# Layer 2 attention of a four-layer kernel: scores as wide products with the mask added on TensorE, and the passes as a loop on each engine

## The reference

```python
q_in = x @ Wq.T                                   # _L2_attn_ref, x already normed
qkv = (q_in @ Wqkv.T + bqkv).reshape(Bs, Ls, 3, Ds)
q, k, v = ...                                     # each (Bs, Ls, G=4 heads, dh=32)
scores = einsum('blgd,bmgd->bglm', q, k) * scale
h = relu(q_in) @ Wop.T
dx_g = (sigmoid(h @ W2.T + b2) * Ls)[:, None] + windows[None, :, None, None]
masked = where(win_mask > dx_g, -BIG, scores)     # win_mask: distance, huge above the diagonal
attn = softmax(masked + scores)
out = einsum('bglm,bmgd->blgd', attn, v)
# _L2_ffn_ref, on the same x
h = silu(lin(x, w1)) * lin(x, w2)
h = gelu(lin(h, h1)); h = gelu(lin(h, h2)); return lin(h, w3)
```

## Time and profile before

| | |
|---|---|
| median of 3 runs | 2189.82 us (2189.76 to 2194.12) |
| the profiled execution | 2189.82 us, span 2188.0 us |
| mean granted TensorE clock | 0.958 |
| layer 2's eight passes | 1216.7 to 1624.1 us |

### The profile page before, as it was taken

How to read it: one execution, slowest core, us unless ns; L and a number is a source line. 1 busy time by engine, 2 the same in 40 slices (tenths; PEclk the granted TensorE clock), 3 DMA queues, 4 the chain that set the end, 5 groups by cost and what they waited for, 6 DMA issues and landing times.

```text
span 2188.0 us, 47512 instructions
## 1 busy us (share of the span) xinstructions
PE 1984.2 (91%) x15804; PEld 1520.2 (69%) x15804; DVE 1491.9 (68%) x5508; ACT 1144.1 (52%) x3575; POOL 901.4 (41%) x1415
## 2 busy tenths in 40 slices
PE   5887887399999999999999899999979999999998
PEld 2555654278887778888777566666657777777776
DVE  6989963366666666666666655556657777777776
ACT  3444352155555555555555454455546666666665
POOL 3113266354554454455445311111125545545544
PEclk9888799699999999999999999999989999999999
DMA  6000016600000000000000000000000000000001
GB/s 189 16 2 1 2 40 168 177 1 2 2 1 2 2 1 1 2 2 1 2 2 1 1 1 1 1 1 1 1 1 2 2 2 1 2 2 2 2 2 40
DMA packets 40592, 37.19 MB, mean 17 GB/s; under 512 B 5664, under 2 KB 38560, under 8 KB 39456
## 3 DMA queue, kind: packets, MB, share of 16 engines
q1 hardware_dynamic: 34720, 29.82, 4.3%
q0 software_dynamic: 5632, 4.33, 1.4%
HBM read 23.53 MB, written 10.62 MB: 16 GB/s over the span
## 4 chain that ended last, share of the span: by engine, by line
PE 56%; DVE 10%; ACT 9%; issue 4%; POOL 3%; DMA 0%; DVEq 0%; POOLq 0%; ACTq 0%
PE bank L1318 7%; PE bank L1307 6%; PE bank L1246 5%; PE bank L1293 5%; PE bank L1290 4%; PE bank L1340 3%; ACT work L1378 3%; PE bank L1231 2%; PE bank L1233 2%; PE bank L1232 2%; PE bank L1310 2%; ACT work L1379 2%; PE bank L1239 2%; PE bank L1786 1%; PE bank L1715 1%
## 5 line engine op out<-in xcount | busy, mean ns | idle before, releaser
L1609 POOL TENSOR_TENSOR work<-work 128x128 f32<-128x128 f32 (+1 forms) x1048 | 506.5, 514 | 659.3 <-DVE work L1526 659.3
L1378 ACT ACTIVATE work<-work 128x128 f32<-128x128 f32 x524 | 206.9, 395 | 513.9 <-DVE work L1514 513.9
L1521 DVE COPY work<-bank 128x384 f32<-128x384 f32 x520 | 283.5, 549 | 21.5 <-PE bank L1318 6.5
L1379 ACT ACTIVATE work<-work 128x256 f32<-128x256 f32 x524 | 258.7, 494 | 0.0
L1318 PE MATMUL bank<-w_const,work 128*128 128x128 f32 x1560 | 227.6, 282 | 1.0 <-POOL work L1609 1.0
L1514 DVE CUSTOM_DVE_ANT_0 work<-bank,mask 128x256 f32<-128x256 f32 x524 | 219.6, 419 | 0.0
L1318 PEld LDWEIGHTS bank<-w_const,work 128*128 128x128 f32 x1560 | 165.8, 141 | 46.2 <-issue 41.8
L1513 DVE CUSTOM_DVE_ANT_0 work<-bank,mask 128x128 f32<-128x128 f32 x524 | 150.5, 287 | 52.3 <-PE bank L1293 48.3
L1307 PE MATMUL bank<-work 128*64 128x256 f32 x1032 | 168.4, 403 | 4.7 <-DVE work L1547 4.3
L1547 DVE COPY work<-bank 128x512 f32<-128x512 f32 x136 | 93.4, 687 | 112.7 <-PE bank L1241 79.4
L1231 PE MATMUL bank<-l_xn_hi,l_qk_hi 128*128 128x256 f32 x532 | 163.4, 307 | 3.0 <-DVE l_xn_lo L1442 2.8
(11 more groups left out here) (335 smaller groups left out, 4883.0 us busy)
## 6 DMA issues: line engine op xcount, KB each, us to landing
w_l<-in_l SPq DMA_DIRECT2D x1, 3210.5 KB, 11.8
w_l<-in_l SPq DMA_DIRECT2D x2, 1540.0 KB, 7.5
w_f<-in_f SPq DMA_DIRECT2D x1, 3072.0 KB, 14.3
x_sb<-in_x SPq DMA_DIRECT2D x4, 512.0 KB, 5.8
normed_rows<-work SPq DMA_DIRECT2D x1, 2048.0 KB, 9.3
even_experts<-x_sb SPq DMA_DIRECT2D x8, 256.0 KB, 3.6
residual<-x_sb SPq DMA_DIRECT2D x1, 2048.0 KB, 9.8
qk<-in_qk SPq DMA_DIRECT2D x2, 1024.0 KB, 8.2
```

The lines of the kernel that those rows point to most:

```text
L1378: act.activation(pr[g % 4][:, Q0], pr[g % 4][:, Q0], ACT.Exp, scale=-1.0, bias=nmx[:, g % 4, 0:1], accum_out=sm[:, g % 4, 0:1])
L1379: act.activation(pr[g % 4][:, Q1], pr[g % 4][:, Q1], ACT.Exp, scale=-1.0, bias=nmx[:, g % 4, 1:2], accum_out=sm[:, g % 4, 1:2]).then_inc(s ...
L1521: dve.tensor_copy(pt[g % 4], PS[2 + g % 2][:, 0:384]).then_inc(s_te.s, 1)
L1609: ins = pool.tensor_tensor(w, w, spread(rc[:, g % 4, q:q + 1], w.shape[1]), ALU.mult)
```

## The change

It touches `layer2()` alone.

- Scores: `kT` becomes `kb`, four blocks of 512 columns, block g with head g's k on its own 32 partitions and zeros elsewhere (POOL writes the zeros once, before the passes). A product of all 128 rows of `qT` with two blocks then gives two heads' scores side by side in one bank. Ahead of them a product of the bf16 unit matrix with the bf16 mask tiles puts the mask into the same bank. A set of scores is six products of 512 columns in banks 0 to 2.
- ACT fills `kb` with four activations of 32 partitions in place of one of 128.
- `maxima` becomes three plain reductions of the banks; `exps` reads the banks. What waited for the end of the maxima, because they had read the banks, waits for the exps now. PE's scores wait for the masks.
- Order: on DVE `masks(1)` and `stats` stand ahead of `maxima(0)`; on PE the turn of x stands ahead of `scores(1)`.
- Banks: the transposes use 3 and 4, the values 5, two middle products 5 and 3, with the waits that belong to them.
- On PE, ACT, DVE and POOL `for i in range(PASSES)` becomes `with engine.Fori(0, PASSES) as i`: one body, run eight times with a branch at its end, each wait's value and the addresses of x's tiles computed in registers.

```diff
-            kT = carve(512)
+            kb = carve(G2, 512)
...
-            MID_BANKS = ((6, 7, 4, 5), (6, 7, 0, 1))
-            TURN_BANKS = (5, 4)
+            MID_BANKS = ((6, 7, 5, 3), (6, 7, 0, 1))
...
-                pe.wait_ge(pre_k, 1)
+                pe.wait_ge(pre_k, 2)
                 pe.wait_ge(pre, 4)
-                for i in range(PASSES):
+                with pe.Fori(0, PASSES) as i:
...
                             if layer == 0 and c == 2:
-                                pe.wait_ge(m_e.s, m_e.at(i, place["k"]))
+                                pe.wait_ge(ot.s, ot.at(i, -1))
+                                pe.wait_ge(d_e.s, d_e.at(i, 0))
                             if layer == 0 and c == 3:
-                                pe.wait_ge(d_e.s, d_e.at(i, 0))
                                 pe.wait_ge(t_e.s, t_e.at(i, -1))
                             if layer == 1 and c == 2:
-                                pe.wait_ge(s_mx.s, s_mx.at(i, 1))
+                                pe.wait_ge(s_ex.s, s_ex.at(i, 1))
...
                     def scores(p):
-                        pe.wait_ge(s_mx.s, s_mx.at(i, p - 1))
-                        if p == 0:
-                            pe.wait_ge(dv.s, dv.at(i, GATED_3))
-                            pe.wait_ge(o_e.s, o_e.at(i, -1))
-                            pe.wait_ge(ot.s, ot.at(i, -1))
-                        for g in range(G2):
-                            r = slice(DH2 * g, DH2 * (g + 1))
-                            pe.matmul(PS[g][:, 0:256], qT[r, p * 256:p * 256 + 128], kT[r, p * 256:(p + 1) * 256], start=True, stop=True, skip_group_check=True)
...
+                        pe.wait_ge(mb_s.s, mb_s.at(i, p))
+                        pe.wait_ge(s_ex.s, s_ex.at(i, p - 1))
+                        pe.wait_ge(o_e.s, o_e.at(i, -1))
+                        for j in range(2):
+                            pe.matmul(PS[j][:, :], ident16[:, :], mb0[p][:, 2 * j:2 * j + 2, :].rearrange("p g k -> p (g k)"), start=True, stop=False)
+                        pe.matmul(PS[2][:, :], ident16[:, :], mb1[p].rearrange("p g k -> p (g k)"), start=True, stop=False)
+                        for j in range(2):
+                            pe.matmul(PS[j][:, :], qT[:, p * 256:p * 256 + 128], kb[:, 2 * j:2 * j + 2, p * 256:(p + 1) * 256], start=False, stop=True)
+                        pe.matmul(PS[2][:, :], qT[:, p * 256 + 128:(p + 1) * 256], kb[:, :, p * 256 + 128:(p + 1) * 256],
+                                  start=False, stop=True).then_inc(s_f.s, 1)
...
-                    scores(1)
-                    pe.wait_ge(f_ig.s, f_ig.at(i, 2))
                     pe.wait_ge(ln_x.s, ln_x.at(i, 0))
                     turn()
+                    scores(1)
...
-                    act.activation(kT, PS[4][:, :], ACT.Identity, bias=L["bk"]).then_inc(m_e.s, 1)
+                    for g in range(G2):
+                        r = slice(DH2 * g, DH2 * (g + 1))
+                        ins_ = act.activation(kb[r, g, :], PS[4][r, :], ACT.Identity, bias=L["bk"][r, :])
+                    ins_.then_inc(m_e.s, 1)
...
+                        act.wait_ge(t_f.s, t_f.at(i, 4 * p + 3 - 8))
                         for g in range(G2):
-                            act.activation(pr0[p][:, g, :], pr0[p][:, g, :], ACT.Exp, scale=-1.0, bias=nmx[:, p, 0, g:g + 1],
+                            act.activation(pr0[p][:, g, :], PS[g // 2][:, g % 2 * 256:(g % 2 + 1) * 256], ACT.Exp, bias=nmx[:, p, 0, g:g + 1],
...
+                    masks(1)
+                    tile = 4 * i + 4
+                    stats(i, tile)
                     def maxima(p):
-                        dve.wait_ge(mb_s.s, mb_s.at(i, p))
                         dve.wait_ge(s_f.s, s_f.at(i, p))
-                        dve.wait_ge(t_f.s, t_f.at(i, 4 * p + 3 - 8))
-                        for g in range(G2):
-                            dve.tensor_tensor_reduce(pr0[p][:, g, :], PS[g][:, 0:256], mb0[p][:, g, :], -1.0, BIG, ALU.add, ALU.min, nmx[:, p, 0, g:g + 1])
...
+                        for j in range(2):
+                            dve.tensor_reduce(nmx[:, p, 0, 2 * j:2 * j + 2], PS[j][:, :].rearrange("p (g k) -> p g k", k=256), AX, ALU.max, negate=True)
+                        dve.tensor_reduce(nmx[:, p, 1, :], PS[2][:, :].rearrange("p (g k) -> p g k", k=128), AX, ALU.max, negate=True).then_inc(s_mx.s, 1)
...
             def pool_(pool):
+                pool.memset(kb, 0.0).then_inc(pre_k, 1)
```

More of the change, by code:

```diff
@@ L1766, in turned @@
                         for c, src in enumerate((pr0[p][:, g, 128:256], pr1[p][:, g, :], pr0[p][:, g, 0:128])):
-                            mm = pe.transpose(PS[TURN_BANKS[n % 2]][:, c * 128:(c + 1) * 128], src, ident)
+                            mm = pe.transpose(PS[(3, 4)[n % 2]][:, c * 128:(c + 1) * 128], src, ident)
                         mm.then_inc(t_f.s, 1)
@@ L1772, in values @@
                         pe.wait_ge(ot.s, ot.at(i, p - 1))
-                        pe.wait_ge(s_mx.s, s_mx.at(i, 1))
                         for g in range(G2):
                             r = slice(DH2 * g, DH2 * (g + 1))
-                            pe.matmul(PS[3][r, 0:256], v_sb[:, 2 * p + 1, r], pt[g][:, 0:256], start=True, stop=False, skip_group_check=True)
+                            pe.matmul(PS[5][r, 0:256], v_sb[:, 2 * p + 1, r], pt[g][:, 0:256], start=True, stop=False, skip_group_check=True)
                         for g in range(G2):
                             r = slice(DH2 * g, DH2 * (g + 1))
-                            pe.matmul(PS[3][r, 0:128], v_sb[:, 2 * p, r], pt[g][:, 256:384], start=False, stop=True,
+                            pe.matmul(PS[5][r, 0:128], v_sb[:, 2 * p, r], pt[g][:, 256:384], start=False, stop=True,
                                       skip_group_check=True).then_inc(pv.s, 1)
@@ L1849, in act_ @@
                 act.activation(xnT, PS[4][:, :], ACT.Copy).then_inc(m_e.s, 1)
-                act.wait_ge(pre_k, 1)
-                for i in range(PASSES):
+                act.wait_ge(pre_k, 2)
+                with act.Fori(0, PASSES) as i:
                     def silu(c):
@@ L1869, in act_ @@
                     act.wait_ge(m_f.s, m_f.at(i, place["k"]))
-                    act.activation(kT, PS[4][:, :], ACT.Identity, bias=L["bk"]).then_inc(m_e.s, 1)
+                    for g in range(G2):
+                        r = slice(DH2 * g, DH2 * (g + 1))
+                        ins_ = act.activation(kb[r, g, :], PS[4][r, :], ACT.Identity, bias=L["bk"][r, :])
+                    ins_.then_inc(m_e.s, 1)
                     def exps(p):
                         act.wait_ge(s_mx.s, s_mx.at(i, p))
+                        act.wait_ge(t_f.s, t_f.at(i, 4 * p + 3 - 8))
                         for g in range(G2):
-                            act.activation(pr0[p][:, g, :], pr0[p][:, g, :], ACT.Exp, scale=-1.0, bias=nmx[:, p, 0, g:g + 1],
+                            act.activation(pr0[p][:, g, :], PS[g // 2][:, g % 2 * 256:(g % 2 + 1) * 256], ACT.Exp, bias=nmx[:, p, 0, g:g + 1],
                                            accum_out=sm[:, p, 0, g:g + 1])
-                            ins_ = act.activation(pr1[p][:, g, :], pr1[p][:, g, :], ACT.Exp, scale=-1.0, bias=nmx[:, p, 1, g:g + 1],
+                        for g in range(G2):
+                            ins_ = act.activation(pr1[p][:, g, :], PS[2][:, g * 128:(g + 1) * 128], ACT.Exp, bias=nmx[:, p, 1, g:g + 1],
                                                   accum_out=sm[:, p, 1, g:g + 1])
@@ L1900, in head_out @@
                 act.wait_ge(pv.s, pv.at(i, 4 * p + 3))
-                act.activation(oT[:, p * 256:(p + 1) * 256], PS[3][:, 0:256], ACT.Identity, bias=L["bv"]).then_inc(ot.s, 1)
+                act.activation(oT[:, p * 256:(p + 1) * 256], PS[5][:, 0:256], ACT.Identity, bias=L["bv"]).then_inc(ot.s, 1)
             def dve_(dve):
@@ L1948, in dve_ @@
                 dve.sem_inc(pre_k, 1)
-                for i in range(PASSES):
+                with dve.Fori(0, PASSES) as i:
                     k[0] = 0
@@ L2008, in turned_out @@
                             dve.wait_ge(pv.s, pv.at(i, n - G2))
-                            dve.tensor_copy(pt[n % G2], PS[TURN_BANKS[n % 2]][:, 0:384]).then_inc(t_e.s, 1)
+                            dve.tensor_copy(pt[n % G2], PS[(3, 4)[n % 2]][:, 0:384]).then_inc(t_e.s, 1)
                     maxima(0)
-                    masks(1)
-                    tile = 4 * i + 4
-                    stats(i, tile)
                     moments()
@@ L2039, in pool_ @@
                     pool.tensor_tensor(lo_w[n], L[w], hi_w[n].bitcast(F32), ALU.subtract).then_inc(pre, 1)
-                for i in range(PASSES):
+                with pool.Fori(0, PASSES) as i:
                     for p in range(2):
```

6 lines of the change are left out of this document (removed).

## The result

| | before | after |
|---|---|---|
| median, same chip | 2194.12 us (5 runs) | 2204.53 us (5 runs, 2201.74 to 2208.14) |
| profiled execution | 2189.82 us, span 2188.0 us | 2205.53 us, span 2203.7 us |
| layer 2, its first product to its last addition | 414.1 us | 427.0 us |
| passes 2 to 7, start to start | 50.75 us | 52.24 us |

The changed kernel is slower by 0.54%, ratio 1.0054 with an interval of 1.0035 to 1.0073: some 10 to 12 us where 35.6 were forecast. The time lies in the whole range (2202 to 2250) but outside the forecast's own 2214 to 2238. The sign is right and the size is not: only a third of the forecast loss came.

The account below looks back on a forecast made before the run. A chain through DVE, ACT and POOL was taken to bound each pass's first half, PE alone the rest. Walk 13.6, register work 4.8, branches 16.8 and start 0.4 add 35.6 to 2189.8: 2225 us, own range 2214 to 2238, whole 2202 to 2250.

Parts of the forecast that it names:

- The branch: At the loop body's end on PE, an instruction fetch exposes 2.4 us, seven times: 16.8 us.
- Rival A: The loop body is kept, so the branches cost only 0.7 us: 2209 us in all; chance 0.27.
- The walk: Following one pass of layer 2 through the engines: it grows by 1.7 us, eight passes by 13.6.
- the set of scores: On PE, three f32 and three bf16 products take 3.5 us a set, 2.6 more than before.
- the turn: PE's turn of the next x, now before the second scores: reached 2.4 us late, taking 0.6 us.
- the second maxima: On DVE they wait for scores, start at 1300.1 and end at 1302.0, 1.7 us late.
- Steps 1: ACT's four k copies and PE's new wait for masks are covered before the first scores, costing 0.1 us.
- 3: On DVE, second masks and statistics go ahead of the first maxima, which start at 1288.3 and take 1.9 us.
- 4: ACT's exps stay 3.6 us, POOL's products end 0.6 us later, and PE's 1.85 us wait for POOL goes.
- The loop's register work: Register operations show at some eight resumes from waits: 0.6 us a pass, 4.8 in all.
- has 4 us to spare: ACT's table load would queue behind the first scores' new wait for masks, with 4 us to spare.
- Before the first pass: POOL's 2.1 us fill of the new k tile precedes the first layer norm's power operation; 0.4 us shows.

Follow-up runs that it names:

- Experiment 1: The kernel before with the passes of PE, ACT and POOL as loops, DVE's still written out; pass 50.78 us, ratio 1.0008.
- experiment 2: The changed kernel with all four engines' loops written out again; pass 51.50 us, ratio 1.0037 to the kernel before.

## Why the forecast was wrong

**The branch: the step that failed.** It was the largest term, 16.8 us, and it measures 0: 0.89 us over the branch against 0.90 without, no packet in six trips. Rival A was the case. The error was to conclude, from packets that are fetched in order, that the earlier ones are not kept: a program without branches shows nothing of what is kept. The Trainium skill ("Runtime: NRT & Kernel Launch", Instruction fetch mechanics) has a taken branch outside a two-page window wait for a DMA; the runs contradict that for the body here. Experiment 1 is the plainest: PE's passes of the kernel before came in 15 packets over seven, a little more than two of 16.7 KB each, so as a loop their start is out of such a window at the end, if narrowly, and the same passes looped brought no packet. The same section gives TensorE's instruction store as 128 KiB; by that number the body is kept, and the trace agrees. I had weighed the one sentence and not the other. The kernel with A's own terms would have been 2209, 3.5 us above the profiled 2205.53; that it comes so near is luck in part, since its walk was 7.6 us too dear, the late table load was missing from it, and 3.3 us of the measured difference arose ahead of layer 2.

**The walk: right in kind, too large.** 1.7 us a pass forecast, 0.75 measured (experiment 2), so 6.0 us instead of 13.6. The mis-sized terms are the set of scores and what follows it. In the unrolled kernel of experiment 2 the second set takes 3.23 us from its first record to the next product, not 3.5: bf16 products of 128x512 start 0.22 apart, as bounded, and f32 ones 0.86 apart. The first set takes 2.83 (15.16 to 17.99 us into the pass), because an fp32r product follows the last f32 one after 0.46 us; but most of that comes back at once, as the product after it starts 0.63 later and not 0.33, as at this place before. PE came to the turn 1.9 late, not 2.4, and the turn took 0.43, not 0.6. So the second maxima began 1.2 late, not 2.0, and they are 1.8 us long, where 1.9 were forecast. (1300.33, with which I compared their end, is where their last record starts before; that is 0.1 of the difference.) Steps 1 (the four copies end at 15.10 in experiment 2 and the scores start at 15.16, 0.13 later than before where 0.1 was forecast), 3 (maxima behind DVE's own queue) and 4 (wait for POOL gone) held.

**The loop's register work: the sum nearly right, its make-up wrong.** 0.6 forecast, 0.74 measured. What is left for register work is 0.33, of it 0.26 at one resume and not spread over eight. The other 0.41 is the late table load, which no term held: I had written that the load "has 4 us to spare", true only where it stands ahead of the wait. That the load stands between the two waits of `exps(0)` was to be seen in the built kernel's order, not in the trace of the kernel before.

**Before the first pass**: layer 2's first product to the first pass took 5.99 us before and 6.13 after, 0.14 against 0.4.

In sum 8 x (0.75 + 0.33 + 0.41) = 11.9 us, beside 12.9 measured over the phase in one profile and 10.4 between the medians. Not settled: how the 0.75 of the walk divides between the scores and the order, and what the last 0.07 of the loops is.

## What to carry to other kernels

Price new work by the idle time that it lands in, and ask first which queue starts the chain: here the same six mask products were worth nothing or 0.96 us a pass. In a loop, put the wait that ends last behind all other waits of its instruction; the others' register additions and a table load then run while the engine stands (0.26 and 0.41 us a pass here). Do not charge a branch for a fetch unless a trace of a loop shows the packets.

## What the runs showed of the hardware

- PE's body, a little more than two packets of 16.7 KB, was not fetched again in six trips (0 packets where the written-out passes had 13), nor was that of any other engine, and the branch took no time that PE's rows show (0.89 us between the products around it, 0.90 without).
- Three waits, two of them with an addition for their value, behind a wait that ends late cost 0.26 us on PE.
- DVE's four small operations on SBUF took 1.12 us alone and 3.42 us beside POOL's tensor products; a split's subtraction took 0.69 us alone, and 1.41 (after) and 2.27 us (before, at 1294.02) beside them.
- A bf16 product of 128x512 costs 0.22 us from start to start, where an fp32r one costs 0.23; an f32 one costs 0.86.
